# All scores of a head pair behind all masks in one run, K's bank for the last columns, context ahead of the scores

## The reference, cut to what matters

```
x = x + 0.5 * moe(layernorm(x))        # 8 experts, top 1, capacity 320, 128 -> 512 -> 128
x = x + attention(layernorm(x))        # 16 heads of 64, causal, tanh after every projection
x = x + 0.5 * moe(layernorm(x))        # the same weights

attention:  q, k, v = tanh(x @ W + b), split into heads
            alpha = softmax(where(causal, q @ k.T / 8, lowest))
            out   = tanh((alpha @ v) @ Wo + bo)
```

## Time and profile before

| | |
|---|---|
| median of three runs | 530.07 us |
| the profiled execution's own time | 530.07 us |
| its span (first to last instruction) | 528.3 us |
| busy: PE, PEld | 416.6 us (79%), 287.9 us (54%) |
| busy: DVE, ACT, POOL | 304.6 us (58%), 254.5 us (48%), 254.4 us (48%) |
| attention, first `qk` to the start of the last | 119.0 to 401.3 us |
| steps i = 4 to 10, each (first Q matmul to the next) | 7.97 us |
| steps r = 3, 4, 5, 6, 7 of batch 1, then r = 0, 1, 2 of batch 2 | 14.84, 8.41, 8.46, 9.75, 8.17, 9.91, 7.98, 7.97 us |

### The profile page before, as it was taken

One profiled execution on the slowest core, in us unless ns is written; L12 is line 12 of the kernel. 1 busy time (PEld: TensorE's weight loads), 2 busy tenths in 40 slices (PEclk: granted clock), 3 DMA queues, 4 the chain that ended last, 5 costly groups with the idle time before them and its releaser, 6 DMA issues.

```text
span 528.3 us, 11673 instructions
## 1 busy us (share of the span) xinstructions
PE 416.6 (79%) x4337; PEld 287.9 (54%) x4337; DVE 304.6 (58%) x926; ACT 254.5 (48%) x441; POOL 254.4 (48%) x277
## 2 busy tenths in 40 slices
PE   1702999409799999999899999899999772299960
PEld 1601777305466766566575666665757442167850
DVE  5872345638967767378864598763888605012213
ACT  1100434007487888477865677684787310034310
POOL 6471245713665565266456565555565520205550
PEclk9999999858799999999999999999999886579995
DMA  7811343172000000000000000000000000125415
GB/s 271 281 54 53 114 134 117 37 257 84 1 2 1 1 4 1 1 2 2 1 2 6 17 2 2 2 1 21 3 2 2 1 20 0 57 59 158 128 53 166
DMA packets 31515, 28.06 MB, mean 53 GB/s; under 512 B 2732, under 2 KB 27365, under 8 KB 31208
## 3 DMA queue, kind: packets, MB, share of 16 engines
q1 hardware_dynamic: 27184, 19.97, 12.6%
q0 software_dynamic: 2560, 4.74, 2.7%
q10 hardware_dynamic: 1720, 2.66, 1.4%
HBM read 16.84 MB, written 10.52 MB: 52 GB/s over the span
## 4 chain that ended last, share of the span: by engine, by line
PE 58%; DVE 15%; POOL 11%; issue 7%; DMA 7%; ACT 1%; POOLq 1%; DVEq 0%; SPq 0%; ACTq 0%
PE sc L697 12%; PE sc L580 7%; PE pj L590 6%; PE pj L667 6%; PE tT L734 4%; POOL disp L330 4%; DVE Ph L1057 3%; PE cx L717 3%; PE cx L719 3%; PE sc L702 3%; PE cx L718 3%; PE pj L677 3%; PE tT L542 3%; DMA ytok<-empty 3%; POOL ytok L341 2%
## 5 line engine op out<-in xcount | busy, mean ns | idle before, releaser
L358 POOL TENSOR_TENSOR Pl<-Pf,Ph 128x512 f16<-128x512 f32 (+1 forms) x64 | 61.9, 980 | 75.4 <-DVE Ph L1057 75.4
L697 PE MATMUL sc<-Tq,Tk 64*128 64x128 f32 (+3 forms) x512 | 96.0, 473 | 0.0
L341 POOL DMA_INDIRECT ytok<-Y,who x48 | 48.6, 1012 | 71.5 <-DVE Y L925 59.2
L358 POOL TENSOR_TENSOR Pl<-Wf,Ph 128x512 f16<-128x512 f32 (+1 forms) x64 | 58.4, 928 | 48.7 <-DVE Ph L1057 48.7
L1057 DVE CAST Ph<-Pf 128x512 f16<-128x512 f32 (+1 forms) x96 | 55.2, 606 | 42.0 <-ACT Pf L491 41.2
L431 ACT ACTIVATE hT<-sc,RT 128x320 f32<-128x320 f32 x64 | 33.8, 528 | 93.2 <-PE sc L580 92.4
L717 PE MATMUL cx<-Vh,Ph 128*128 128x65 f16 x640 | 66.9, 197 | 14.5 <-POOL Vl L358 10.3
L717 PEld LDWEIGHTS cx<-Vh,Ph 128*128 128x128 f16 x640 | 59.9, 99 | 16.7 <-POOL Vl L358 11.5
L718 PE MATMUL cx<-Vl,Ph 128*128 128x64 f16 x640 | 67.0, 195 | 0.0
L719 PE MATMUL cx<-Vh,Pl 128*128 128x65 f16 x640 | 66.7, 195 | 0.0
L1057 DVE CAST Ph<-Wf 128x512 f16<-128x512 f32 (+1 forms) x96 | 53.7, 591 | 19.6 <-ACT Wf L491 19.1
(11 more groups left out here) (179 smaller groups left out, 842.6 us busy)
## 6 DMA issues: line engine op xcount, KB each, us to landing
W<-in_L_ffn_w SPq DMA_DIRECT2D x32, 256.0 KB
disp<-empty SPq DMA_DIRECT2D x2, 1290.0 KB, 7.7
XE<-disp SPq DMA_DIRECT2D x16, 129.0 KB
ytok<-empty SPq DMA_DIRECT2D x2, 1024.0 KB, 12.7
G<-ytok SPq DMA_DIRECT2D x8, 256.0 KB, 4.0
out<-X SPq DMA_DIRECT2D x4, 256.0 KB, 2.4
ytok<-Y,who POOLq DMA_INDIRECT x48
XE<-disp SPq DMA_DIRECT2D x16, 32.2 KB
```

Of the source, the lines that this page charges most:

```text
L341: pool.indirect_dma_start(ytok[phase], bass.IndirectOffsetOnAxis(ap=who[u][0:m, j:j + 1], axis=0), Y[u][0:m, j, :], None).then_inc(y_sc[u] ...
L358: pool.tensor_tensor(dst, src, hi, ALU.subtract).then_inc(done, 1)
L697: mm(score_bank(h, c)[:, o:o + w], Tk[u][half(h), P * kt:P * kt + P], Tq[u][half(h), P * kt:GN], start=kt == kts[0], stop=False)
```

## The change

- PE: `context` of head 0 goes in front of the scores. All scores of a pair are one run: first the 8 mask matmuls for all banks (they now carry `start`), then 14 score matmuls (before 8) in the 64-row form, cut so that both heads have the same number of columns (1280) and write different banks at any time. Chunk 2 of both heads goes to bank pj1, K's projection bank. The mask part waits for all exponentials of the pair before and for K's tanh of this step (`tk`, s + 2); a wait of PE on its own count (`s_ps`) keeps the heads apart in pj1; `qk` waits for all six exponentials of pair i-2 before it writes pj1.
- ACT: `v_high` from the end of the step to behind the two tanh; exponentials in the order `ORDER`: chunk 0 of head 0 and 1, chunk 1 of head 1 and 0, tanh of V, chunk 2 of head 0 and 1.
- DVE: casts and subtractions alternate; DVE does the three subtractions of head 0 (512, 512, 256 columns) where before it did chunk 1 of both heads; both `normalise` stand in front of them.
- POOL: the three subtractions of head 1 (before: four, 512, 512, 256, 256 columns), with `v_low` in front of them.
- The router's small matmuls of a batch go to sc0 and sc1, the last output projection to pj0.

```diff
 ROW = P + 1
+SCORED = [(0, 0), (0, 1), (2, 0), (1, 1), (1, 0), (2, 1)]
+ORDER = [(0, 0), (0, 1), (1, 1), (1, 0), (2, 0), (2, 1)]
 E = 8
...
 CHUNKS = [(0, 512, [0]), (512, 512, [1, 3]), (1024, 256, [2])]
-ORDER = [(c, h) for c in range(3) for h in range(2)]
-POOL_LOWS = [(0, 0), (0, 1), (2, 0), (2, 1)]
-V_LOWS = [(1, 0), (1, 1)]
 
...
         def low_part(s, h, c):
 
-            done, lows = ("p_lo_p", POOL_LOWS) if (c, h) in POOL_LOWS else ("p_lo_v", V_LOWS)
-            return S[done], len(lows) * s + lows.index((c, h)) + 1
+            mine = [k for k, g in ORDER if g == h]
+            return S["p_lo_p" if h else "p_lo_v"], 3 * s + mine.index(c) + 1
+
+        def done_by(s, h, c):
+            return 6 * s + ORDER.index((c, h)) + 1
+
+        def scored_by(s, h, c):
+
+            return 6 * s + (6 if c == 2 else SCORED.index((c, h)) + 1)
 
         def score_bank(h, c):
-            return sc[2 * h + (c == 1)]
+            return pj1[:, 256 * h:256 * h + 256] if c == 2 else sc[2 * h + c]
+
+        batch_logits, batch_ranks = sc[1], sc[0]
...
             def p_low(s, u):
-                for c, h in POOL_LOWS:
-                    a, n, _ = CHUNKS[c]
-                    pool.wait_ge(S["p_hi"], 6 * s + 2 * c + h + 1)
-                    low(Pl[u][h][:, a:a + n], Pf[u][h][:, a:a + n], Ph[u][h][:, a:a + n], S["p_lo_p"])
+                for c, (a, n, _) in enumerate(CHUNKS):
+                    pool.wait_ge(S["p_hi"], done_by(s, 1, c))
+                    low(Pl[u][1][:, a:a + n], Pf[u][1][:, a:a + n], Ph[u][1][:, a:a + n], S["p_lo_p"])
 
             def step(b, r, score=True, between=None):
                 i, u = NPAIR * b + r, r % 2
                 if between:
                     between()
                 if score:
+                    v_low(i - 1, 1 - u)
                     p_low(i - 1, 1 - u)
-                    v_low(i - 1, 1 - u)
...
+                act.wait_ge(S["s_ps"], scored_by(s, h, c))
+                if s >= 2:
+                    act.wait_ge(*low_part(s - 2, h, c))
+                act.activation(Pf[u][h][:, a:a + n], score_bank(h, c)[:, 0:n], ACT.Exp, scale=0.125,
+                               bias=pshift[:]).then_inc(S["exp_done"], 1)
...
                     between()
                 if score:
-                    exps(i - 1, 1 - u, 0)
-                    exps(i - 1, 1 - u, 1)
+                    v_high(i - 1, 1 - u)
+                    for c, h in ORDER[:4]:
+                        exps(i - 1, 1 - u, c, h)
                 if project:
                     tanh_v(i, u)
                 if score:
-                    exps(i - 1, 1 - u, 2)
+                    exps(i - 1, 1 - u, *ORDER[4])
+                    exps(i - 1, 1 - u, *ORDER[5])
                 if turn:
                     copy_ct(i - 3, (r - 3) % NPAIR)
-                if score:
-                    v_high(i - 1, 1 - u)
...
-                first = isinstance(i, int) and i == 0
                 if r == 0:
                     pe.wait_ge(S["x_lo"], b + 1)
-                if not first:
+                if i:
                     pe.wait_ge(S["tv"], i)
                 for w, ps, done in ((0, pj0, "q_ps"), (1, pj1, "k_ps")):
-                    if w and not first:
-                        pe.wait_ge(S["tk"], i)
-                    if w and r == 0 and not first:
-                        pe.wait_ge(S["rank_read"], NS + b - 1)
+                    if w and i == 1:
+                        pe.wait_ge(S["tk"], 1)
+                    if w and i >= 2:
+                        pe.wait_ge(S["exp_done"], 6 * (i - 2) + 6)
                     for t, (wl, xl) in enumerate(TERMS):
                         last = mm(ps[:], wpart(w, wl, r), (XL if xl else XH)[:, bass.ds(GN * b, GN)],
...
-            def scores(s, u, c, bank_read=None):
-
-                first = isinstance(s, int) and s == 0
-                if c == 0:
-                    pe.wait_ge(S["tq"], s + 1)
-                    pe.wait_ge(S["tk"], s + 1)
-                if c == 2:
-                    pe.wait_ge(S["exp_done"], 6 * s + 2)
-                elif not first:
-                    pe.wait_ge(S["exp_done"], 6 * (s - 1) + (6 if c == 0 else 4))
-                if bank_read:
-                    pe.wait_ge(*bank_read)
-                a, n, kts = CHUNKS[c]
-                for kt in kts:
-                    o, w = KOFF[kt] - a, GN - P * kt
+            def scores(s, u, project):
+
+                if s:
+                    pe.wait_ge(S["exp_done"], 6 * s)
+                if project:
+                    pe.wait_ge(S["tk"], s + 2)
+                for c, (a, n, kts) in enumerate(CHUNKS):
                     for h in range(2):
-                        mm(score_bank(h, c)[:, o:o + w], Tk[u][half(h), P * kt:P * kt + P], Tq[u][half(h), P * kt:GN],
-                           start=kt == kts[0], stop=False)
+                        for kt in kts:
+                            o = KOFF[kt] - a
+                            mm(score_bank(h, c)[:, o:o + P], identb[:], maskn[:], start=kt == kts[0] and not (c == 2 and h),
+                               stop=False)
+                pe.wait_ge(S["tq"], s + 1)
+                pe.wait_ge(S["tk"], s + 1)
+
+                def part(h, c, kt, x, y, last=False):
+                    o, q = KOFF[kt] - CHUNKS[c][0], P * kt
+                    m = mm(score_bank(h, c)[:, o + x:o + y], Tk[u][half(h), q:q + P], Tq[u][half(h), q + x:q + y],
+                           start=False, stop=last and (c, h) != (2, 0))
+                    if last:
+                        m.then_inc(S["s_ps"], 1)
+
                 for h in range(2):
-                    for kt in kts:
-                        o = KOFF[kt] - a
-                        last = mm(score_bank(h, c)[:, o:o + P], identb[:], maskn[:], start=False, stop=kt == kts[-1])
-                    last.then_inc(S["s_ps"], 1)
+                    part(h, 0, 0, P, GN)
+                for h in range(2):
+                    part(h, 0, 0, 0, P, True)
+                part(0, 2, 2, 0, P)
+                part(1, 1, 1, 0, P)
+                part(0, 2, 2, P, 2 * P, True)
+                part(1, 1, 1, P, 3 * P)
+                part(0, 1, 1, 0, P)
+                part(1, 1, 3, 0, P, True)
+                part(0, 1, 1, P, 3 * P)
+                pe.wait_ge(S["s_ps"], 6 * s + SCORED.index((2, 0)) + 1)
+                part(1, 2, 2, 0, P)
+                part(0, 1, 3, 0, P, True)
+                part(1, 2, 2, P, 2 * P, True)
 
             def context(c, u, h):
                 if h == 0:
                     pe.wait_ge(S["v_lo"], c + 1)
-                pe.wait_ge(S["p_hi"], 6 * c + h + 5)
-                pe.wait_ge(*low_part(c, h, 2))
-                pe.wait_ge(*low_part(c, h, 1))
+                pe.wait_ge(S["p_lo_p" if h else "p_lo_v"], 3 * c + 3)
                 if h or not (isinstance(c, int) and c == 0):
...
@@ -765,26 +783,25 @@
                     if turn:
                         tt_free(i - 3)
                     early()
-                if score:
-                    scores(i - 1, 1 - u, 0)
-                    scores(i - 1, 1 - u, 1, c1_read)
                 if mix:
                     context(i - 2, u, 0)
+                if score:
+                    for read in score_reads:
+                        pe.wait_ge(*read)
+                    scores(i - 1, 1 - u, project)
                 if project:
                     v(i, b, r)
-                if score:
-                    scores(i - 1, 1 - u, 2)
                 if turn:
                     if tt_read:
                         pe.wait_ge(*tt_read)
                     context_t(i - 3, 1 - u)
                 if late:
-                    pe.wait_ge(S["tk"], i + 1)
+                    pe.wait_ge(S["exp_done"], done_by(i - 1, 0, 0))
                     late()
                 if mix:
                     context(i - 2, u, 1)
                 if end:
-                    pe.wait_ge(S["exp_done"], 6 * (i - 1) + 3)
+                    pe.wait_ge(S["exp_done"], done_by(i - 1, 0, 1))
                     end()
...
-                c1_read = {7: (S["dl_ready"], NS + b)}
+                late = {7: lambda: rank_batch(b - 1, batch_ranks)}
+                end = {6: lambda: route_logits(b - 1, batch_logits)}
+                score_reads = {7: [(S["dl_ready"], NS + b)], 0: [(S["rank_read"], NS + b - 1)] if b > 1 else []}
                 for r in range(NPAIR):
                     step(b, r, early=early.get(r), late=late.get(r), end=end.get(r),
-                         c1_read=c1_read.get(r), tt_read=tt_read.get(r))
-
-            step(NG, 0, project=False)
+                         tt_read=tt_read.get(r), score_reads=score_reads.get(r, ()))
+
+            step(NG, 0, project=False, score_reads=[(S["rank_read"], NS + NG - 1)])
             pairs = NPAIR * NG
-            pe.wait_ge(S["rank_read"], NS + NG - 1)
-            project_out(NG - 1, pj1, 0, 6)
+            pe.wait_ge(S["tv"], pairs)
```

(29 more changed lines are left out.)

34 lines of the change are left out of this document (8 added, 26 removed).

## The result

The changed kernel takes 591.09 us (median of four runs, 588.31 to 593.43), the kernel before beside it 529.62 (four runs, 526.89 to 533.33): a ratio of 1.117, interval 1.112 to 1.122. It is slower by 61.5 us, 12%. The profiled execution has a span of 591.7 us and took 593.43.

The account below looks back on a forecast made before the run. PE's own list was taken to bound the attention before (40.00 of 40 us busy). Forecast: 530.1 + 48 for the new loop + 12 for the clock = 590 us, 8 in 10 range 555 to 612.

Parts of the forecast that it names:

- What bounds it, and the loop: PE bounds the attention before; the change closes a loop from head 0's context through scores, exponentials, splits and normalise back.
- The saving on PE: Three 64-row score visits become one: 0.59 us less a step, 0.17 given back for K's tanh, 7.55 us of work.
- The walk of the loop: Middle step, context to next context: 7.73 us without memory exclusions between DVE and POOL, 9.80 with them, 1.83 more.
- The other steps: Steps of a batch with router or output projection work: -0.5 to +3.5 us each; a whole batch +12.6.
- The sum of the loop: All steps of the run: 12.8 for i = 4 to 10, 25.2, 6.3 and about 3.5 us, together +48.
- The clock: PE's clock falls to half behind long idle times, 11.5 times at about 1 us each: +12 us.
- rival 2: PE's clock falls in nearly all steps: 615 us; chance 0.12.
- Rival 1: Only DVE's casts meet POOL, or DVE lets POOL in once a step: 8.8 us a step, 549 us; chance 0.12.
- Rival 3: The loop doesn't bind and PE stays the bound, each step gaining 0.42 us: 517 us; chance 0.03.
- rival 5: Only partly covered exclusions between DVE and POOL cancel the gain: about 530 us; chance 0.04.
- a step below 9 us: First Q matmul to the next under 9 us: the sign that the forecast is wrong and rival 1 holds.
- Rival 4: PE's saving isn't there and the short score records are slower, 0.9 us a run: about 596 us, inside the forecast.

Follow-up runs that it names:

- experiment 1: The changed kernel with the context of head 0 moved back behind the whole score run: 558.49 us, ratio 1.056 to the kernel before.
- Experiment 4: The kernel before with chunks 0 and 1 as one score run behind their masks, two visits instead of three: 524.51 us, ratio 0.998; repeated, 524.19 us, 0.996.
- experiment 2: The changed kernel with POOL's subtractions cut to 16 columns each, the other low parts left out: 527.16 us, ratio 0.996 to the kernel before.
- experiment 3: The changed kernel with matmuls nobody reads put in PE's idle time before the context of head 0: 578.92 us, ratio 1.094 to the kernel before.
- experiment 6: The changed kernel with the single score run undone, four visits with masks behind each: 575.20 us, ratio 1.094 to the kernel before.
- experiment 5: The changed kernel with DVE's normalise of head 1 moved ahead of its second subtraction: 547.57 us, ratio 1.036 to the kernel before.

## Why the prediction was right

It gave 590 us, and 591.09 was measured. Step by step:

- **What bounds it, and the loop.** Right. The idle time in front of the context of head 0 is 2.15 us (forecast 2.3), 29 waits for DVE's product make 68.2 us, and experiment 1, which moves that context back, takes off 32 of 61.5 us.
- **The saving on PE.** The sum is right, its two terms are not, and they cancel: luck. The prediction had 7.97 - 0.59 + 0.17 = 7.55 us of work a step, the 0.17 for a wait for K's tanh. The trace has 7.55 us without such a wait: in the middle steps the masks follow the context with no idle time, so nothing is given back, and two visits fewer saved 0.42 us, or 0.21 each. Experiment 4 says the same with 0.23 for one. (Two small readings do not come out either, and nothing hangs on them: 2.30 - 2.20 is 0.10 and not 0.17, and the inputs of head 0's context had been ready for 0.83 us, since POOL's low part of V ends at 204.02, and not for 0.6.) The score run is 2.39 us long, with no loss in the short records, as forecast. Since the loop binds, none of this moves the total.
- **The walk of the loop.** A full-clock step takes 9.70 us, forecast 9.80; the first exponential stands 2.60 us behind the context, forecast 2.61. The exclusions were needed: without them the walk gave 7.73, and experiment 2, where they are all but gone, has 7.92. The Trainium skill's rule (SBUF — State Buffer, Who interferes with whom), that a DVE instruction with two SBUF inputs contends with a GpSimd instruction that reads SBUF, was what made me apply them to DVE's subtractions, which no row of the kernel before showed beside POOL's except once. The trace now shows them, in both directions: 1.53 instead of 0.69 us on DVE, 1.54 instead of 1.16 on POOL. The rule gives no price; the rows do.
- **The other steps, at full clock (experiment 3).** r = 3: 14.26, forecast 14.3. r = 4: 9.77 (9.80). r = 5: 11.10 (12.0). r = 6 and 7 together: 20.2 (19.9). r = 0: 12.63 (12.5). A batch: 87.4 us against 75.5 before, +11.9, forecast +12.6. The miss is r = 5, where I put all of the statistics behind the loop.
- **The sum of the loop.** i = 4 to 10: 7 x (9.70 - 7.97) = 12.1 (forecast 12.8); two batches 23.7 (25.2); the last, r = 3 to 7, 5.7 (6.3). That is 41.5 where the forecast had 44.3. What is left of 61.5 - 15 is about 5 for the steps at the ends, forecast 3.5 (the first Q matmul of i = 4 is 4.4 us later than before). Together 46.5, forecast 48.
- **The clock.** The weakest term, and under-sized: 15 us, forecast 12. The number of falls was right (ten of the 27 steps from i = 4 to 30; forecast 11.5 in all), and rival 2 (nearly all steps) was wrong. The price of one was not: 11.3 - 9.7 = 1.6 us in a middle step, 1.7 to 2.7 in r = 5 and 2.6 to 2.8 in r = 0, where I had said about 1. The half-speed stretch does not end with the first scores: in the windows above it lasts about 3.4 us, until 195.2, 4 us after the start of the context. The ten falls sum up to 20.5 us, and some 5 of these come back: several of the steps that follow one are 0.2 to 0.9 us shorter than the same steps in experiment 3.
- **So the total came out closer than its terms:** the loop 1.5 us too high, the clock 3 too low.
- **PE's busy share.** I wrote "down to some 75%"; it is 33.13 of 40, 83%, since half-speed work counts as busy. By the step at full clock it is 7.55 / 9.70 = 78%. In the chain that ended last DVE grew from 15% to 24% and ACT from 1% to 4%, as forecast; POOL fell from 11% to 6%, which I had the wrong way round.
- **The rivals.** Rival 1 (casts alone meet POOL, 8.8 us a step) fell with the row of 1.53 us. Rival 3 (PE stays the bound) and rival 5 (it cancels) needed the loop to be under 8 us; only experiment 2 reached that, with most of POOL's work left out, and it gained 0.4%. The sign "a step below 9 us" did turn up once from i = 4 on (8.96, right after the step of 15.44 us), but with the clock kept up (experiment 3) the middle steps take 9.7 us. Rival 4 (slower short records) fell with the 2.39 us.

## What to carry to other kernels

Before an order on the bounding engine is changed to save its time, walk the loop that the new order closes through the other engines, with every wait and every shared resource in it: here 0.4 us saved a step bought a loop of 9.7 us where the engine needed 7.55. Work that stands in front of the first result of such a loop is paid for: the masks and the cut in front of the first exponential cost 0.28 us of the 0.29 by which a middle step is longer than in experiment 6, while 1.4 us more of PE work elsewhere in the step cost it nothing. Look also at which small waits a longer run puts in front of all its parts (the router's, in experiment 1). And when a small saving on the bounding engine does not show, look at the few irregular steps first: moving one block of DVE behind its splits, in two steps of 32 and the last, turned a gain of some 0.3% into one of about 1.5%.

## What the runs showed that I had not expected

- The clock after equal idle times. Behind 2.14 and 2.15 us, at the same place of two following steps, it fell once (0.64 in the next 2.4 us) and once not (1.00), and from i = 4 to 10 steps of 11.3 us and of 9.3 to 9.7 us took turns. The idle time alone does not decide it. Behind 1.35 us (experiment 5) and 0.98 us (experiment 1) it never fell in a middle step.
- Filling the idle time with matmuls that nobody reads made the changed kernel some 12 us faster (experiment 3), and doing the scores in a form that costs PE 1.4 us a step more made it 12 us faster as well (experiment 6).
- A fall of the clock costs much more than the 1 us I had put down: 1.6 us in a 9.7 us step, 2.6 to 2.8 in r = 0.
- The router's reads in front of the whole score run cost experiment 1 17.6 us in six waits, which no trace of the changed kernel showed, since its wait for the loop comes first.
